# Attention in groups of four heads, with the exponentials turned by VectorE in 32x32 blocks

## What is computed

```python
xn = layernorm(x)
# attention: 16 heads of 64
h = rmsnorm(xn, norm_scale)
q, k, v = h @ wq, h @ wk, h @ wv                # per head; q * 64 ** -0.5
w = softmax(q @ k.T, axis=-1)                   # 512 x 512 per batch and head
attn = sum over heads of (w @ v) @ w_out[head] + b_out
# experts: 128 -> 512 -> 128, top 2 of 8
logits = silu(xn @ rw1 + rb1) @ rw2 + rb2
p = softmax of the two largest logits
ffn = sum over the two of p * (silu(xn @ w1[e] + b1[e]) @ w2[e] + b2[e])
out = x + attn + ffn
```

## Time and profile before

| | |
|---|---|
| median of 3 runs | 2018.02 us |
| profiled execution, its own time | 2015.25 us |
| its span, first to last instruction | 2013.4 us |
| TensorE busy | 1946.6 us (97%) |
| VectorE busy | 1538.4 us (76%) |
| ScalarE busy | 1574.0 us (78%) |
| GpSimd busy | 918.5 us (46%) |
| mean granted TensorE clock | 0.989 of full |

### The profile page before, as it was taken

How to read it: one execution, slowest core, us unless ns; L and a number is a source line. 1 busy time by engine, 2 the same in 40 slices (tenths; PEclk the granted TensorE clock), 3 DMA queues, 4 the chain that set the end, 5 groups by cost and what they waited for, 6 DMA issues and landing times.

```text
span 2013.4 us, 45217 instructions
## 1 busy us (share of the span) xinstructions
PE 1946.6 (97%) x16646; PEld 1256.0 (62%) x16646; DVE 1538.4 (76%) x2654; ACT 1574.0 (78%) x3716; POOL 918.5 (46%) x790
## 2 busy tenths in 40 slices
PE   7999999999999999998899999999999999999997
PEld 5666656565666656555566666666666666666664
DVE  6888888888888888877677777777777777777775
ACT  6777777777777777775588888888888888888885
POOL 4244455453344344431024646445446455454454
PEclk9999999999999999998899999999999999999999
DMA  2023232211111111110323334333433333343332
GB/s 85 28 62 107 91 101 91 83 67 41 40 40 44 42 41 43 34 38 28 102 68 80 85 85 84 87 81 84 87 80 85 85 80 92 81 84 82 80 75 47
DMA packets 132697, 141.96 MB, mean 71 GB/s; under 512 B 25438, under 2 KB 99038, under 8 KB 132446
## 3 DMA queue, kind: packets, MB, share of 16 engines
q1 hardware_dynamic: 101886, 118.34, 18.6%
q0 software_dynamic: 30592, 20.73, 8.7%
HBM read 102.65 MB, written 38.46 MB: 70 GB/s over the span
## 4 chain that ended last, share of the span: by engine, by line
PE 78%; ACT 11%; DVE 4%; issue 3%; DMA 2%; another core or an unknown queue 0%; SPq 0%; POOL 0%; POOLq 0%; ACTq 0%; DVEq 0%
PE pair L380 22%; PE pair L348 16%; PE pair L363 11%; PE pair L275 7%; PE pair L277 5%; PE pair L276 5%; ACT PR L1024 4%; PE pair L292 3%; PE pair L399 3%; PE pair L401 3%; PE pair L522 1%; PE pair L523 1%; PE pair L521 1%; DVE NM L646 1%; ACT V L1046 1%
## 5 line engine op out<-in xcount | busy, mean ns | idle before, releaser
L1024 ACT ACTIVATE PR<-pair,NM 128x512 f32<-128x512 f32 x1024 | 717.8, 721 | 19.5 <-DVE NM L646 17.5
L646 DVE TENSOR_REDUCE NM<-pair 128x2 f32<-128x1024 f32 x512 | 611.5, 1211 | 48.1 <-PE pair L348 43.5
L1038 ACT COPY PT<-pair 128x512 f32<-128x512 f32 x640 | 357.8, 607 | 350.7 <-PE pair L363 350.7
L348 PE MATMUL pair<-KS,QS 64*128 64x512 f32 x3072 | 491.1, 423 | 14.9 <-DVE KS L639 10.5
L380 PE MATMUL pair<-PT,V 128*64 128x512 f32 x2048 | 471.7, 603 | 0.2
L363 PEld LDWEIGHTS pair<-idn,PR 64*128 64x128 f32 x8192 | 337.5, 139 | 99.9 <-ACT HS L1072 26.2
L348 PEld LDWEIGHTS pair<-KS,QS 64*128 64x128 f32 x3072 | 257.3, 188 | 176.0 <-issue 129.5
L363 PE MATMUL pair<-idn,PR 64*128 64x64 f32 x8192 | 342.5, 223 | 21.2 <-ACT HS L1072 15.6
L1302 POOL TENSOR_TENSOR HH<-ZZ,HH 128x512 fp32r<-128x512 f32 x156 | 199.2, 1347 | 291.4 <-ACT HH L1123 291.4
L1309 POOL DMA_INDIRECT out<-YS,IDW x156 | 247.0, 1584 | 186.4 <-DVE YS L933 127.9
L380 PEld LDWEIGHTS pair<-PT,V 128*64 128x64 f32 x2048 | 136.5, 137 | 259.4 <-issue 253.5
(11 more groups left out here) (166 smaller groups left out, 2809.5 us busy)
## 6 DMA issues: line engine op xcount, KB each, us to landing
E<-w_tab SPq DMA_DIRECT2D x78, 512.0 KB
RB<-l_rows SPq DMA_DIRECT2D x127, 256.0 KB
XG<-slots SPq DMA_DIRECT2D x39, 264.0 KB
w_tab<-SPL SPq DMA_DIRECT2D x16, 512.0 KB
l_rows<-RT SPq DMA_DIRECT2D x508, 1.0 KB
xin<-in_x SPq DMA_DIRECT2D x16, 256.0 KB
XQ<-in_x SPq DMA_DIRECT2D x16, 256.0 KB
RAW<-in_w SPq DMA_DIRECT2D x16, 256.0 KB, 8.1
```

The lines of the kernel that those rows point to most:

```text
L348: m = pe.do.matmul(bank[bk + j], a[half[j], cols], c[half[j], :], start=(k == 0), stop=(k == 2))
L646: dve.do.tensor_reduce(NM[:, 2 * t:2 * t + 2], pairs[BANK["S", n, t] // 2][:], AX.X, ALU.max, negate=True).then_inc(sem["dve_max"])
L1024: act.do.activation(PR[:, k, :], bank[BANK["S", n, t] + j], ACT.Exp, bias=NM[:, k:k + 1], accum_out=RS[:, n % 2, j, t:t + 1]).then_inc(sem ...
L1038: act.do.copy(dst[r], src[r]).then_inc(sem["act_PT"])
```

## The change

Attention now goes by groups of four heads, 64 groups of four ticks (G = 4 g + k), eight steps to a group, two to a tick. A step is 64 queries of all four heads, that is as many scores as before.
- `scores`: Q and K are kept as plain fp32 (no low halves). A step is eight fp32 matmuls of 64 rows by 32 columns, each in its own corner of the array, again into two banks. The two pairs of banks 0 to 3 serve the scores alone, in turn, so step s waits for the exponentials of step s - 2.
- `probs`: as before, but into two buffers `PR`; step s waits for the turn of step s - 2.
- `turn_probs`: no TensorE transposes and no copies; DVE turns 128x1024 in 32x32 blocks from `PR` straight into `PT` (a ring of 12 steps). On DVE the order is maximum of step 2k, turn of step 2k - 1, maximum of 2k + 1, turn of 2k, the tick's other work.
- `weighted`: 32-row by 64-column fp32 tiles with 256 columns moving, eight corners, 128 matmuls per group, half in tick k = 0 and half in k = 1 of the next group; it takes all four of the banks 4 to 7. V therefore goes to DRAM (`v_rows`) and comes back as `V4` with keys in 32-row blocks.
- `OT`, `WO`: once per group, DVE in tick k = 2 between two maxima, TensorE's `project_out` in the same tick. V, K and Q of the next group are projected in ticks k = 2 and 3, and ACT alone copies them out.
- All other work shares banks 4 to 7 in plain rotation (`Ring`). Experts stand in ticks k = 2 and 3 only: per two tiles three such ticks, t0 (output of the tile before, input of tile i), t1 (turn of i + 1, output of i), t2 (input of i + 1). The fourth chunk's halves stand first in the following tick on DVE, ACT and POOL.

```diff
--- before.py
+++ after.py
+GH = 4
+STEPS = 8
+RING = 12
-PE_ORDER = [
-    "S0 T0 S1 T1 kq spread attend ahead weighted experts route".split(),
...
-TURN_ON = [["act", "act"], ["dve", "act"], ["act", "act"], ["dve", "dve"]]
...
-class Banks:
+class Ring:
...
+    def take(self, use):
+        self.of[use] = GH + self.used % GH
+        self.used += 1
+        return self.of[use]
...
-        V = sb("V", [P, QT, H * DH])
-        QS = sb("QS", [P, 2, 2, S], F32R)
-        KS = sb("KS", [P, 2, 2, S], F32R)
-        PR = sb("PR", [P, 8, S])
-        PT = sb("PT", [P, 4, QT, S])
+        VS = sb("VS", [P, 2, 512])
+        V4 = sb("V4", [P, 2, S // 32, 2 * DH])
+        QS = sb("QS", [P, 2, 2, S])
+        KS = sb("KS", [P, 2, 2, S])
+        PR = sb("PR", [P, 2, 2, S])
+        PT = sb("PT", [P, 2, S // 32, 32 * RING])
...
+        def tick(j):
+            return FIRST if j == 0 else FIRST + 3 + (j - 1) // 2 * 4 + (j - 1) % 2
...
+            for tile, G in ((i, t0), (i + 1, t2)):
+                if tile < NT:
+                    if tile == i + 1:
+                        PLAN[G].append((i, "back"))
+                    PLAN[G] += [(tile, "h", c) for c in range(NC)]
+                    AHEAD[G + 1] += [(tile, "halves", 3)]
+            if i + 1 < NT:
+                PLAN[t1].append((i + 1, "turn"))
+            PLAN[t1].append((i, "y"))
...
+            def scores(g, s):
+                step = STEPS * g + s
+                at = 32 * place_of(g, s)[1]
+                pe.wait_ge(sem["act_k"], 2 * g + 2)
+                pe.wait_ge(sem["act_q"], 2 * g + 2)
+                pe.wait_ge(sem["act_exp"], 2 * step - 2)
+                for c in range(4):
+                    for r in range(2):
+                        rows = slice(DH * r, DH * r + DH)
+                        cols = slice(c // 2 * 256 + at, c // 2 * 256 + at + 32)
+                        m = pe.do.matmul(bank[2 * (s % 2) + r][32 * c:32 * c + 32, :], QS[rows, g % 2, c % 2, cols],
+                                         KS[rows, g % 2, c % 2, :], start=True, stop=True, tile_position=(DH * r, 32 * c))
                 m.then_inc(sem["pe_S"])
...
-            def turn_probs(n, t):
-                two = [banks.take("T", ("T", n, t, r)) for r in range(2)]
...
+            def weighted(g, half):
+                if half == 0:
+                    pe.wait_ge(sem["dve_tr"], STEPS * g + STEPS)
+                    pe.wait_ge(sem[f"V4_{g % 2}"], 64 * (g // 2 + 1))
+                    for a in range(GH):
+                        came_free(GH + a)
+                for k in range(8 * half, 8 * half + 8):
+                    for c in range(2):
+                        for a in range(GH):
...
+                            m = pe.do.matmul(bank[GH + a][DH * c:DH * c + DH, 0:256], V4[rows, g % 2, k, DH * c:DH * c + DH], moving,
+                                             start=(k == 0), stop=(k == 15), tile_position=(32 * a, DH * c))
...
+            def project_out(g):
+                bk = ring.take(("OP", g))
+                p = g % 4 * 2
+                pe.wait_ge(sem["dve_OT"], 2 * g + 2)
...
+            for G in range(TIMES + 4):
+                g, k = divmod(G, 4)
+                if g < GROUPS:
+                    scores(g, 2 * k)
+                    scores(g, 2 * k + 1)
+                if k < 2 and 0 < g <= GROUPS:
+                    weighted(g - 1, k)
+                attending(G)
+                experts(G)
+                route(G)
...
+            def turn_probs(g, s):
+                step = STEPS * g + s
+                slot = place_of(g, s)[0]
+                dve.wait_ge(sem["act_exp"], 2 * step + 2)
+                if step >= RING:
+                    dve.wait_ge(sem["pe_PV"], (step - RING) // STEPS + 1)
+                dve.do.transpose(PT[:].rearrange("p c k q -> p (c k) q")[:, :, 32 * slot:32 * slot + 32],
+                                 PR[:, step % 2].rearrange("p r k -> p (r k)")).then_inc(sem["dve_tr"])
...
+                g, k = divmod(G, 4)
+                for i, _, c in AHEAD[G]:
+                    halves(i, c)
+                if g < GROUPS:
+                    maxima(g, 2 * k)
+                if k or 0 < g <= GROUPS:
+                    late = STEPS * g + 2 * k - 1
+                    if late < STEPS * GROUPS:
+                        turn_probs(late // STEPS, late % STEPS)
+                if k == 0 and 0 < g <= GROUPS:
+                    denominators(g - 1)
+                if k == 2 and 0 < g <= GROUPS:
+                    weighted(g - 1)
+                if g < GROUPS:
+                    maxima(g, 2 * k + 1)
+                    turn_probs(g, 2 * k)
+                if k == 2 and 0 < g <= GROUPS:
+                    project_out(g - 1)
+                attending(G)
+                experts(G)
+                route(G)
...
+                for i, _, c in AHEAD[G]:
+                    halves(i, c)
+                if g < GROUPS:
+                    probs(g, 2 * k)
+                    probs(g, 2 * k + 1)
+                attending(G)
+                splitting(G)
+                experts(G)
+                route(G)
...
+                    sp.do.dma_start(V4[32 * a:32 * a + 32, g % 2], v_rows[half % 2][g % 2 * 2 + a % 2]).then_inc(sem[f"V4_{g % 2}"], 16)
```

More of the change, by code:

```diff
@@ L385, in spread @@
[L385 to L396 removed]
+                free[bk] = sem["act_" + name], n + 1
@@ L1063, in router, with attending @@
+            def attending(G):
+                gr, k = divmod(G, 4)
+                if k >= 2 or gr == 0:
+                    half, t = divmod(2 * gr + k + 2, 4) if k >= 2 else (0, 2 * k)
+                    for u in (t,) if k >= 2 else (t, t + 1):
+                        if half < 2 * NB:
+                            values(half, u)
+                if k >= 2 and gr + 1 < GROUPS:
+                    project(2 * gr + k, True)
+                    project(2 * gr + k, False)
             def router(r, c):
@@ L1482, in experts @@
             def experts(G):
-                for i, what, *c in parts_of(G, PLAN):
-                    if what == "rows" and i >= 2:
-                        fetch_rows(i)
-                    if what == "in" and i:
-                        fetch_weights(i, 0)
-                    if what == "out" and i:
-                        fetch_weights(i, 1)
+                for i, what, *c in PLAN[G - 1] if G else ():
+                    if what == "turn" and i + 2 < NT:
+                        fetch_rows(i + 2)
+                for i, what, *c in PLAN[G]:
+                    if what == "h" and c[0] == 3 and i + 1 < NT:
+                        fetch_weights(i + 1, 0)
+                    if what == "y" and i + 1 < NT:
+                        fetch_weights(i + 1, 1)
             load_x(0)
```

746 lines of the change are left out of this document (268 added, 478 removed), and 3 rows, old and new, of the table HOLD.

## The result

| | before | after |
|---|---|---|
| median of its runs | 2018.8 us (2014.8 to 2020.4, 4 runs) | 2732.0 us (2720.9 to 2746.8, 4 runs) |
| profiled run: own time, span | 2015.25, as shown ahead | 2746.8, 2745.0 |
| granted clock, mean | 0.989 | 0.875 |

The ratio to the kernel before is 1.354 (95% interval 1.347 to 1.361). The forecast was 2425 us, with 2140 to 2760 as its range: the direction came true and so, in the main, did the mechanism; the size was 307 us too small.

What follows compares the result with a forecast made beforehand. TensorE's remaining work and its waits for inputs were taken as the bound. Start 24, first half 1002, groups before experts and change-over 90, experts 1155, end 26 make 2297; clock 128 gives 2425 us, range 2140 to 2760.

Steps and rivals of the forecast that it cites:

- Operations: Durations on DVE and TensorE: long turn 1.24 us, half of PV 3.6 us, step of scores 0.95 us.
- Rivals 1 (half rate) and 2 (corners in turn): DVE turns take 2.3 us, 2730 us total, chance 0.07; array corners not all abreast, 3120 us, chance 0.05.
- Rival 4: TensorE runs empty at each change of corner size, 115 us more, 2540 us total; chance 0.05.
- k = 0, wait for the eighth turn: First tick: PV waits for the turn behind the new maximum on DVE; TensorE idles 1.5 us, tick 7.2 us.
- k = 1: Second tick: 5.5 us, or 7.4 with the router's small DVE operations in every other first-half group; mean 6.45.
- k = 2, wait for `OT`: Third tick: `project_out` waits for `OT` behind a maximum and a turn; TensorE idles 2.7 us, tick 10.0 us.
- k = 3: Fourth tick: scores wait for ACT's K and Q copies behind both exponentials; idle some 2.2 us, tick 7.6 us.
- The experts: Second half, k = 2 and 3: ACT's input work and POOL's transfers and low halves make groups 39.5 us on average.
- The clock: TensorE's idle gaps lower its clock: 2.0 us per group, bounds 0 and 4, 128 us in all.
- Rivals 3 and 5: TensorE's clock stays up, 2297 us, chance 0.13; the waits are not on the path, 1770 us, chance 0.10.

Runs made afterwards that it cites:

- e3: Changed kernel with DVE's product giving `OT` ahead of the k = 2 tick's first maximum and late turn instead of behind them: 2537.4 us, ratio 1.261.
- e6: As e3, with the turn of each tick's last step ahead of the next tick's first maximum on DVE: 2435.9 us, ratio 1.208.
- e5: As e3, with five of POOL's eight indirect transfers per block moved from beside PV to beside scores and projections: 2492.2 us, ratio 1.238.
- e10: As e3, plus the edits of e5, e6 and e7, fourth chunk behind first maximum and exponentials, V, K, Q copies between k = 3's exponentials: 2298.9 us, ratio 1.150.
- e2: As e3, with three unused matmuls on TensorE before PV's wait and three before the first scores' wait: 2557.6 us, ratio 1.270.
- e7: As e3, with the experts' low halves computed on DVE instead of POOL, each behind the next chunk's product: 2503.0 us, ratio 1.244.
- e1: Changed kernel with V stored and reloaded through DRAM for the first two groups alone, later PV using old V: 2718.6 us, ratio 1.351.

## Why the prediction was right, and where 307 us went

**What bounds it.** Right: little TensorE work left, and a chain of fixed orders in its place. The page shows 75% busy, and e3 and e6, which change nothing but an order on DVE, take 195 and 101 us back. Where the length of a group was missed, by ticks (us, from the start of a tick's scores to that of the next tick's; means of groups 1 to 31, and of the ticks from 139 on, with experts):

| | forecast | measured |
|---|---|---|
| first half: k = 0, 1, 2, 3 | 7.2, 6.45, 10.0, 7.6 | 8.8, 8.5, 12.3, 8.1 |
| experts: k = 0 and 1, then k = 2 and 3 | 13.7, 25.8 | 18.5, 29.5 |

**Operations.** Right to a few per cent: the turn 1.230 us (1.24), half of PV 3.64 from start to start (3.6), a step of scores 0.94 (0.95), `project_out` 0.86 at full clock. So the straight line from a 128x32 turn held up to 1024 columns, in fp32. The 311 ns that the prediction took from the Trainium skill ("VectorE: DVE Perf Modes", The three transpose paths) are for bf16; that they gave the same 1.24 us was not to be counted on. Rivals 1 (half rate) and 2 (corners in turn) are out.

**Rival 4, the pause between shapes.** I held the logits' row of the kernel before against it, but a recorded time includes the way through the engine, so an overlap of 0.07 us proves nothing; what counts is from start to start, and from the last transpose to the logits that is 0.15 us, against 0.06 between pairs of transposes. At full clock one pass of 512 columns follows another after 0.43 us (`project_out` 0.86 for two). Here are the last pass of a tick's scores and the first of PV (TensorE, cut out of the group above):

```profile
545.68 0.64 PE L315 MATMUL pair<-KS,QS 64*32 64x512 f32 x8
546.25 0.47 PE L333 MATMUL pair<-PT,V 32*64 32x256 f32 x8
```

They start 0.57 us apart, 0.14 more than a pass, and so it is at full clock wherever no wait stands between. From PV to scores it is 0.35 in place of 0.22, from scores to V's projection 0.57, and in the kernel before 0.53 in place of 0.43 from PV to scores; between matmuls of one shape nothing is added. So TensorE does pause at a change of shape, for 0.10 to 0.14 us. The forecast did not go wrong by it: its 0.95 and 3.6 us leave room for it, as two passes of 0.43 are 0.86 us and 16 of 0.216 are 3.46. Rival 4's 115 us on top of them are out. The rule in the Trainium skill ("TensorEngine Tiling (Array Packing)", Key Properties), that such a change drains the engine, agrees with this, with 0.10 to 0.14 us as its price.

**k = 0, wait for the eighth turn.** Mechanism right, size right in the first half: 27.4 us in 16 groups between 300 and 900 us, 1.7 each (forecast 1.5). Wrong in the second: 113.7 us in 23 groups between 1500 and 2600 us, 4.9 each. The forecast had the fourth chunk ahead of this maximum in one group of three, for 2.9 us. It is there in two of three, and the waits repeat as 5.3, 9.5 and 1.7 us (TensorE, three groups):

```profile
2065.60 5.10 PE L333 MATMUL pair<-PT,V 32*64 32x256 f32 x128 [5.32 <-DVE PT L577]
...
2111.83 5.87 PE L333 MATMUL pair<-PT,V 32*64 32x256 f32 x128 [9.48 <-DVE PT L577]
...
2161.01 3.71 PE L333 MATMUL pair<-PT,V 32*64 32x256 f32 x128 [1.68 <-DVE PT L577]
```

**k = 1.** The router's small operations were weighed here (7.4 us in every other group). The runs show nothing of it: where PV is not stretched the tick is 5.5 us, with or without them (5.5 on the mean in e5). The 8.5 us come from the long halves. The operations cost their time in k = 2 instead, where I had taken them off the books, as the chain of waits of the changed kernel shows:

```profile
550.20 0.08 DVE gm L689
550.30 0.20 DVE gt L691
...
552.30 0.04 DVE PM L715
...
552.38 1.22 DVE NM L569
```

They run to 552.3, the first step of the tick's scores has been ready since some 550.9, and the next maximum, turn and `OT` are later by that.

**k = 2, wait for `OT`.** Right in place and releaser (64 times), 3.1 us against 2.7: 2.9 us in most groups, 4.1 where the router's operations run. The rest of this tick's miss is the clock: behind the gap each half of `project_out` takes up to 1.7 us in place of 0.86.

**k = 3.** Right in size in the first half, wrong in the waiter. The scores hardly wait for ACT (25.6 us of idle before L315 in all, 13.5 of it for copies of K and Q). TensorE stops earlier in the tick: the router's and the experts' matmuls need a bank of the ring, and it comes free with ACT's copy of V, which stands behind both exponentials. That is 174 us in 55 waits, nearly all in k = 3: 2.0 us per group up to the change-over and 3.8 with experts, against 2.2. Two of them (TensorE):

```profile
570.18 0.50 PE L244 MATMUL pair<-XT,R 128*128 128x512 f32 x1 [1.76 <-ACT VS L918]
...
2151.32 1.08 PE L261 MATMUL pair<-idn,XG 128*128 128x128 f32 x4 [5.80 <-ACT VS L918]
```

e10, which moves the copies, brings 0.5 us per group.

**The experts.** The largest miss, 8.6 us per group with the clock in it. In k = 2 and 3 the forecast had TensorE wait 6.3 us in one group of three for POOL's low halves; it does so six times in all, for some 7 us, and waits for ACT's copy of V more often than that. DVE's price of the fourth chunk was read from a trace in which POOL's low halves hardly ever ran beside it. Ahead of the 9.5 us wait they do (DVE, then POOL):

```profile
2102.19 0.69 DVE L815 SCALAR_TENSOR_TENSOR ZZ<-ZT,ZZ 128x512 f32<-128x512 f32 x1 [0.49 <-ACT ZZ L984]
...
2104.88 4.61 DVE L815 SCALAR_TENSOR_TENSOR ZZ<-ZT,ZZ 128x512 f32<-128x512 f32 x1
2109.41 1.21 DVE L569 TENSOR_REDUCE NM<-pair 128x2 f32<-128x1024 f32 x1
```

```profile
2104.65 4.28 POOL L1162 TENSOR_TENSOR HH<-ZZ,HH 128x512 fp32r<-128x512 f32 x3
```

The same product takes 0.69 us alone and 4.61 beside three of POOL's subtractions, and the maximum, the turn and PV are queued behind it.

**The clock.** This is the term that was mis-sized for the whole program. I counted 1.2 falls of the clock per group at 1.7 us each, 128 us in all. The trace has 136 separate stretches at the lower level, 2.1 per group and 689 us together; TensorE was busy in 540 us of them, so 270 us of its work was put off, 2.0 us each. It was the number of falls that was wrong, more than their price; the 4.2 us per group lie just above the upper bound of 4. Not all of it is on the path: e2 lifted the clock by 0.026 and gained nothing. How much is on it was not settled.

**The long halves of PV**, 100 us in k = 1, were in no term at all.

The parts (clock 270 - 128 = 142 us beyond the forecast, the wait before PV in the second half some 29 x 2.4 = 70, ZZ 79, long halves 100, `OT` 0.4 x 64 = 26) make 417 us where 322 are to be explained; they overlap, since a wait hides what falls into it and the long halves run in part at the lower clock. The runs price four orders and places (195 us for e3 against the changed kernel; 101, 45 and 34 for e6, e5 and e7 against e3), not these parts' shares of the 322. That the result lies inside the range, 28 us below its upper end, is in part the width of the range: the long halves, the colliding products and the number of clock falls were not foreseen.

**Rivals 3 and 5.** The clock did not stay. The waits were on the path: with six orders and places changed the ratio fell from 1.354 to 1.150, part of which is the missing of long halves where e10 ran.

## What to carry to other kernels

Where one engine at 97% loses a part of its work to another at 76%, ask first for the order on the second: here the whole set of reductions, turns and products fits (DVE is at 65%), and what costs is that each waits in line behind one whose input is not there yet. An operation whose input is long ready belongs ahead of one that waits for the engine that is to be fed. And a duration read off beside an idle neighbour is not the duration beside a busy one.

## What was not expected of the hardware

- **DVE and POOL slow each other.** ZZ (two inputs, all in SBUF) takes 0.69 us alone, and in the 56 cases with more than 0.3 us of POOL's subtraction beside it 2.1 us on the mean, up to 5.0; the subtraction takes 1.41 alone and 1.69 beside ZZ. The copy ZZ to HH takes 0.43 alone and 1.39 beside it (20 cases). Turns (1.23 us with or without it, 41 cases beside it) and sums with an input in PSUM (`X`, 0.69, 15 cases) are untouched. The Trainium skill ("Advanced Engine Details and Errata", GPSIMD Details) says that POOL shares a read and a write interface with DVE, in conflict with operations that have two SBUF inputs or run in a two-port mode; the rows of ZZ agree, and they add the size; in what mode the copy ran no run shows.
- **A stream of small matmuls can be stretched by POOL's indirect transfers**: 128 records in 8 to 12 us in place of 3.7, gone when the transfers stand elsewhere (e5), unchanged by 97 MB less traffic (e1), and absent where the kernel before ran at 2001 us. The kernel before shows nothing of it, neither in PV (16 records of 512 columns in that time) nor in its transposes (16 records of 64 columns in 0.66 us), but there only two transfers stand in a row, not five. Why is open.
- **Corners of rows and columns of fp32 run abreast at full rate**: eight 32x64 corners of 256 columns every 0.216 us, eight 64x32 corners of 512 columns every 0.43.
- **A change of tile shape costs TensorE 0.10 to 0.14 us**, in both kernels (under rival 4 above).
